# Product-key stage: five small fp32 matmuls get zero rows and unused columns to fill the array

## What is computed

```python
q = (x @ Wq).reshape(b, n, HEADS, DIM) * DIM ** (-0.5)
kv_scores, indices = _pk(x, Wq_pk, pk_keys)      # softmax of the 16 best of 4096 key pairs per token and head
k = jnp.einsum('bnhk,bnhkd->bnhd', kv_scores, keys_table[ind])
v = jnp.einsum('bnhk,bnhkd->bnhd', kv_scores, values_table[ind])
sim = jnp.einsum('bihd,bjhd->bhij', q, k)        # then a causal mask
attn = jax.nn.softmax(sim, axis=-1)
out = jnp.einsum('bhij,bjhd->bhid', attn, v)     # then @ Wo, and added to h
```

## The kernel before

| line | before: rows used, stationary columns, moving columns |
|---|---|
| 1768 | 64 (partitions 64 to 127), 121, 64; twice |
| 1769 | 64, 64, 242 |
| 1775 | 64, 121, 121 and 242 |
| 1801 | 64, 121, 128; four times |
| 1808 | 121, 8, 121 |

## Time and profile before

### The profile page before, as it was taken

How to read it: one execution, slowest core, us unless ns; L and a number is a source line. 1 busy time by engine, 2 the same in 40 slices (tenths; PEclk the granted TensorE clock), 3 DMA queues, 4 the chain that set the end, 5 groups by cost and what they waited for, 6 DMA issues and landing times. The chain is left out here.

```text
span 13713.0 us, 173171 instructions
## 1 busy us (share of the span) xinstructions
PE 9379.0 (68%) x41773; PEld 6076.6 (44%) x41773; DVE 8471.7 (62%) x30632; ACT 5332.5 (39%) x12786; POOL 2229.0 (16%) x2261
## 2 busy tenths in 40 slices
PE   2596799985977999999999999998981010001000
PEld 2486677763863544444444444444971000000000
DVE  7656787665777888888888888886657311111112
ACT  2463466652534555555555555554540000000000
POOL 0000000000000000000000000000000677777774
PEclk6797899997988999999999999998985555555555
DMA  0000000000003333333333333332000432222222
GB/s 5 4 1 2 11 1 4 1 3 2 1 7 90 95 93 98 95 94 93 99 93 95 93 99 93 95 93 58 1 3 19 58 23 22 22 22 26 24 21 39
DMA packets 453151, 616.44 MB, mean 45 GB/s; under 512 B 167514, under 2 KB 420979, under 8 KB 431758
## 3 DMA queue, kind: packets, MB, share of 16 engines
q1 hardware_dynamic: 377490, 566.32, 17.0%
q0 software_dynamic: 74592, 38.28, 4.6%
HBM read 369.09 MB, written 44.81 MB: 30 GB/s over the span
## 5 line engine op out<-in xcount | busy, mean ns | idle before, releaser
L1812 PE MATMUL pm_out<-pm_w,pm_tab 128*128 128x484 f32 x8192 | 4018.1, 571 | 0.9 <-DVE pm_w L2056 0.2
L1917 ACT ACTIVATE pm_e<-pm_sums 128x484 f32<-128x484 f32 x4096 | 2318.4, 574 | 1525.5 <-PE pm_sums L1827 1511.4
L2056 DVE SCALAR_TENSOR_TENSOR pm_w<-pm_sums,pm_e 128x484 f32<-128x484 f32 x4096 | 2661.9, 651 | 148.4 <-ACT pm_e L1917 131.7
L2741 POOL DMA_INDIRECT g_got<-gat_sources,ed_idx x2048 | 1982.5, 968 | 690.4 <-issue 674.3
L1812 PEld LDWEIGHTS pm_out<-pm_w,pm_tab 128*128 128x128 f32 x8192 | 1561.7, 192 | 968.9 <-issue 623.6
L2749 PE MATMUL g_ps<-k_ident,g_xs 121*128 121x121 f32 x32 | 10.7, 437 | 2501.9 <-DVE g_xs L2865 2501.9
L1827 PE MATMUL pm_sums<-pm_mv,pm_pick 96*128 96x484 bf16 x4096 | 1518.3, 371 | 44.9 <-DVE pm_w L2056 24.7
L2878 DVE TENSOR_TENSOR g_e<-g_got,g_b 128x512 f32<-128x512 f32 x16 | 11.1, 692 | 1814.4 <-DMA g_got<-gat_sources,ed_idx 1814.3
L2749 PEld LDWEIGHTS g_ps<-k_ident,g_xs 121*128 121x128 f32 x32 | 5.1, 182 | 2505.1 <-DVE g_xs L2865 2505.0
L113 POOL TENSOR_TENSOR xn<-h,s_st 121x1024 f32<-121x1024 f32 x1 | 2.9, 2937 | 5483.6 <-DVE s_st L94 5483.6
L2810 ACT ACTIVATE g_ex<-g_ex 128x1024 f32<-128x1024 f32 x16 | 16.9, 1056 | 2188.6 <-DVE g_ex L2893 2188.6
(11 more groups left out here) (563 smaller groups left out, 18280.1 us busy)
## 6 DMA issues: line engine op xcount, KB each, us to landing
pm_tab<-in_L_ffn_tables SPq DMA_DIRECT2D x128, 2048.0 KB, 8.0
pm_mv<-pm_parts SPq DMA_DIRECT2D x3072, 60.5 KB, 2.4
g_got<-gat_sources,ed_idx POOLq DMA_INDIRECT x2048, 2.6
pm_gb<-pk_threshold_rows SPq DMA_DIRECT2D x128, 242.0 KB, 7.7
gat_running<-g_rec SPq DMA_DIRECT2D x16, 1536.0 KB, 5.7
gat_expert_rows<-g_y SPq DMA_DIRECT2D x32, 242.0 KB
g_y<-gat_expert_rows SPq DMA_DIRECT2D x4, 1936.0 KB
gat_heads<-ed_same SPq DMA_DIRECT2D x4, 1024.0 KB
```

What stands on the lines that cost most here:

```text
L1812: pe.matmul(out[:, hd % 2, 0:CHUNK], tab[hd % 2][:, t, :], w[:, t % NW, :], start=(t == 0), stop=(t == KT - 1)).then_inc(used, 1)
L1917: a.activation(e[:, t % NW, :], sums[:, t % NB, 0:CHUNK], ACT.Exp).then_inc(exp_ready, 1)
L2056: v.scalar_tensor_tensor(out=w[:, t % NW, :], in0=sums[:, t % NB, 0:CHUNK], scalar=0.0, in1=e[:, t % NW, :], op0=ALU.is_gt, op1=ALU.mult). ...
L2741: g.indirect_dma_start(got[c][:, w, :], None, rows, bass.IndirectOffsetOnAxis(ap=idx[:, i * W + w:i * W + w + 1].bitcast(U32), axis=0)).th ...
```

## The change

Tiles whose matmuls used 64 rows get 128 partitions: `sw`, `xa`, `xc` and `q`. `wo` had 128 already and used its upper half. The added halves are set to zero once, by new memsets in the two `load_all` calls; `wq` gets 64 more columns and `tg` is 128 columns wide instead of 8. The matmuls of the five lines then take all 128 partitions of both operands, or (1808) all 128 columns. Where only one side is zero in the added rows, the other holds finite numbers of another use: `kv` has keys in its lower and values in its upper half. Line 1769 now writes 128 output partitions, of which the upper 64 hold the next head's columns and are read by nobody. All other instructions, their order and their waits stay.

```diff
-        sw = outer.enter_context(nc.sbuf_tensor("pk_sw", [C, NH, 2 * NK], F32))
+        sw = outer.enter_context(nc.sbuf_tensor("pk_sw", [128, NH, 2 * NK], F32))
...
-                [(bd[:, :, :], 0.0)], norm=(k["norm"], h, xn))
+                [(bd[:, :, :], 0.0), (sw[C:128, :, :], 0.0)], norm=(k["norm"], h, xn))
...
-            xb, xa, gb, xc = sb("xb", [KD, CHUNK]), sb("xa", [C, CHUNK]), sb("gb", [128, CHUNK]), sb("xc", [C, CHUNK])
+            xb, xa, gb, xc = sb("xb", [KD, CHUNK]), sb("xa", [128, CHUNK]), sb("gb", [128, CHUNK]), sb("xc", [128, CHUNK])
...
-            tg, tgT, tick = sb("tg", [TP, 2 * TT]), sb("tgT", [2 * TT, TP]), sb("tick", [1, 16])
-            wq, wo = sb("wq", [C, NH * C]), sb("wo", [128, NH, C])
+            tg, tgT, tick = sb("tg", [TP, 128]), sb("tgT", [2 * TT, TP]), sb("tick", [1, 16])
+            wq, wo = sb("wq", [128, NH * C + C]), sb("wo", [128, NH, C])
...
-            q = [sb(f"q{c}", [C, T]) for c in both]
+            q = [sb(f"q{c}", [128, T]) for c in both]
...
-                [(keys[:, :, :], 0.0)])
+                [(ap, 0.0) for ap in (keys[:, :, :], wq[:, :], wo[0:C, :, :], xa[:, :], xc[:, :], tg[:, :], q[0][:, :], q[1][:, :])])
...
                             for t in range(NT):
-                                pe.matmul(X[0:TP, 256 + t * C:256 + (t + 1) * C], kv[c][C:2 * C, t * TP:(t + 1) * TP], wo[C:2 * C, hd, :], start=True, stop=True)
-                            pe.matmul(X[0:C, 0:T], wq[:, hd * C:(hd + 1) * C], xa[:, c * T:(c + 1) * T], start=True, stop=True).then_inc(step[c], 1)
+                                pe.matmul(X[0:TP, 256 + t * C:256 + (t + 1) * C], kv[c][:, t * TP:(t + 1) * TP], wo[:, hd, :], start=True, stop=True)
+                            pe.matmul(X[:, 0:T], wq[:, hd * C:hd * C + 128], xa[:, c * T:(c + 1) * T], start=True, stop=True).then_inc(step[c], 1)
...
                             for t in range(NT):
-                                ins = pe.matmul(Y[0:TP, KEYS[t]], q[c][:, t * TP:(t + 1) * TP], kv[c][0:C, 0:(t + 1) * TP], start=True, stop=True)
+                                ins = pe.matmul(Y[0:TP, KEYS[t]], q[c][:, t * TP:(t + 1) * TP], kv[c][:, 0:(t + 1) * TP], start=True, stop=True)
...
-                        pe.matmul(out[0:2 * TT, bank, 0:TP], tg[:, :], ident[0:TP, 0:TP], start=True, stop=True).then_inc(FI, 1)
+                        pe.matmul(out[:, bank, 0:TP], tg[:, :], ident[0:TP, 0:TP], start=True, stop=True).then_inc(FI, 1)
...
-                            a.activation(q[c][:, :], X[0:C, 0:T], ACT.Copy)
+                            a.activation(q[c][0:C, :], X[0:C, 0:T], ACT.Copy)
```

More of the change, by code:

```diff
@@ L1446, in _ @@
                     a.wait_ge(folded, 1)
-                    a.activation(sw[:, :, :].rearrange("p (b n) k -> p b (n k)", b=2), ps[0][0:C, 0:2, :], ACT.Copy)
+                    a.activation(sw[0:C, :, :].rearrange("p (b n) k -> p b (n k)", b=2), ps[0][0:C, 0:2, :], ACT.Copy)
             xT = sb("xT", [C, M])
@@ L1515, in _ @@
                                 ins = pe.matmul(ps[c][0:TP, 2 * t + q, :], xT[:, c * T + t * TP:c * T + (t + 1) * TP],
-                                                sw[:, 4 * q:4 * q + 4, :].rearrange("p n k -> p (n k)"), start=True, stop=True)
+                                                sw[0:C, 4 * q:4 * q + 4, :].rearrange("p n k -> p (n k)"), start=True, stop=True)
                         ins.then_inc(step[c], 1)
@@ L1629, in stage_l2_ffn @@
                 (mask[:, 0:TP], k["causal"][:, 0, 0:TP]), (mask[:, TP:3 * TP], k["causal"][:, 1, :]), (picks[:, :, :], k["picks"]),
-                (wq[:, :], A["L2_ffn_Wq"]), (wo[C:2 * C, :, :], A["L2_ffn_WoH"].rearrange("n p c -> p n c")),
-                (tab[0][:, :, :], A["L2_ffn_tables"][0]), (xa[:, :], x_rows[:, 0:CHUNK]),
+                (wq[0:C, 0:NH * C], A["L2_ffn_Wq"]), (wo[C:2 * C, :, :], A["L2_ffn_WoH"].rearrange("n p c -> p n c")),
+                (tab[0][:, :, :], A["L2_ffn_tables"][0]), (xa[0:C, :], x_rows[:, 0:CHUNK]),
                 (xb[0:C, :], x_rows[:, 0:CHUNK]), (xb[C:KD, :], t_rows[0, 0:1, 0:CHUNK]),
-                (xc[:, :], x_rows[:, CHUNK:2 * CHUNK])],
-                [(keys[:, :, :], 0.0)])
+                (xc[0:C, :], x_rows[:, CHUNK:2 * CHUNK])],
+                [(ap, 0.0) for ap in (keys[:, :, :], wq[:, :], wo[0:C, :, :], xa[:, :], xc[:, :], tg[:, :], q[0][:, :], q[1][:, :])])
             sums_ready, exp_ready = sem("sums_ready"), sem("exp_ready")
@@ L1727, in body @@
                                 sp.sem_inc(passed, 1)
-                                sp.dma_start(xc[:, :], x_rows[:, CHUNK:M][:, bass.ds(ck * CHUNK, CHUNK)]).then_inc(xc_loaded, 16)
+                                sp.dma_start(xc[0:C, :], x_rows[:, CHUNK:M][:, bass.ds(ck * CHUNK, CHUNK)]).then_inc(xc_loaded, 16)
                             if more:
@@ L1755, in body @@
                                 sp.sem_inc(xa_free, 1)
-                                sp.dma_start(xa[:, :], x_rows[:, bass.ds(ck * CHUNK, CHUNK)]).then_inc(xa_loaded, 16)
+                                sp.dma_start(xa[0:C, :], x_rows[:, bass.ds(ck * CHUNK, CHUNK)]).then_inc(xa_loaded, 16)
                     chunks(sp, body, lambda g, ck: None)
@@ L1985, in _ @@
                     v.tensor_copy(pick[:, :, :], picks[:, :, :]).then_inc(setup, 1)
-                    v.tensor_copy(keys[0:C, :, :], sw[:, :, :])
+                    v.tensor_copy(keys[0:C, :, :], sw[0:C, :, :])
                     v.memset(keys[C:KD, :, NK:2 * NK], 1.0).then_inc(setup, 1)
```

## The result

The changed kernel takes 13478.8 us (median of 4 runs, 13478.2 to 13486.9) against 13704.7 us: a ratio of 0.9836, 95% interval 0.9823 to 0.9849. That is 226 us less; 238.5 were forecast, and the time lies inside the range. The span of the profiled execution is 13476.7 us, 236 less than that of before. The two profiled executions already differ by 12 us ahead of the first added memset (the one before it, of `pk_bd`, starts at 4011.33 and at 3999.39 us), where nothing was changed. So the medians are the better measure of the whole, and the loop's own length that of the edit.

A forecast was written before the change was run, and what follows sets the result against it. TensorE was taken to bound the product-key loop. Savings of 183 us (`q`, `s`) and 59 us (the other two groups), 242 together, less 3.5 us of memsets, gave 238.5 off 13705.3: 13467 us, range 13452 to 13502.

The forecast's parts named there:

- TensorE sets the pace: Product-key loop: TensorE is busy 994 of 1000 us, so every us its stream gains or loses moves the end.
- The cost sits at the edges: Small matmul groups: 0.09 to 0.10 us is paid on entering a group using part of the array, none for full ones.
- The prices of the full array: Four small groups: `q` saves 0.42 us, `s` 0.29 to 0.30, `next_scores` 0.29, `turn_thresholds` 0.20; together 242 us.
- 4 x 0.097 + 2 x 0.203: Group `q`, lines 1768 and 1769: four short records plus two of 242 columns, 0.80 us against 1.22.
- The poor value: Group `q` with paces of 0.11 and 0.21 us: 0.86 us, saving 0.36.
- Nobody takes it back: VectorE's mask waits, 1.13 and 2.51 us, cover TensorE's savings of 0.72 and 1.21; VectorE goes on waiting at every mask.
- The race at t=12: TensorE already waits 0.10 us at t=12, read as for VectorE's `w`; should keep 0.10 us; if lost, 13543 us.
- The memsets: Added before the loads, all on the path: 3.5 us more (2.5 to 5), of which `sw` 0.9.
- Loads stay hidden over all rows: Rival: full-row weight loads wait for the matmul before them, each record pays its load, 13918 us; 2 in 100.
- The granted clock: Rival: filled rows lower TensorE's granted clock to 0.9 in the loop, 560 us on, 14027 us; 1 in 100.
- It doesn't do what it says: Rival: gap comes from output shape or fp32 with few columns, zero rows change nothing, memsets stay: 13709 us; 2 in 100.
- Half of it: Rival: only inner pace improves, 13588 us, or VectorE's race at t=12 is lost, 13543 us; 5 in 100 together.

The follow-up runs named there:

- next_to_s: Kernel before, no tile changed, `next_scores` moved from t=20 to t=21, directly behind lane 1's `s`: 13862.8 us against 13905.3, ratio 0.9970.
- query_first: Changed kernel with line 1769 written before line 1768 in `q`: 13670.1 us against 13907.0 for the kernel before on its chip, ratio 0.9829.
- s_only: Kernel before with the full array for line 1775 (`s`) alone, upper half of `q` tiles zero: 13836.0 us against 13905.3, ratio 0.9950.
- turn_only: Kernel before with line 1808 alone changed, 128 stationary columns instead of 8: 13884.5 us against 13905.3, ratio 0.9984.

## Why the prediction was right, and what was mis-sized

- **TensorE sets the pace**: right. Busy share and waits of the earlier trace rows carried through: the gain of TensorE's stream, 232 us by the groups, is the gain of the loop, 231.4 us.
- **The cost sits at the edges**: right, and next_to_s shows it apart from the zero rows. The entry is 0.09 to 0.10 us, which the prediction read in the earlier trace rows; the rest of the 0.29 us of a group it only priced as a whole. The traces divide it. First `s` in the kernel before, with the weight load (PEld) and, from a view cut so that it begins there, the third record; then the same in the changed kernel:

```profile
6020.91 0.49 PEld L1775 LDWEIGHTS pm_y<-pm_kv,pm_q 64*121 64x121 f32 x4 [0.71 <-issue]
6021.22 0.57 PE L1775 MATMUL pm_y<-pm_kv,pm_q 64*121 64x242 f32 x2
6021.73 0.38 PE L1827 MATMUL pm_sums<-pm_mv,pm_pick 96*128 96x484 bf16 x1
```

```profile
6013.74 0.18 PEld L1775 LDWEIGHTS pm_y<-pm_kv,pm_q 128*121 128x121 f32 x1 [0.22 <-issue]
6014.35 0.57 PE L1775 MATMUL pm_y<-pm_kv,pm_q 128*121 128x242 f32 x2
```

At the edge the first load begins only with its record (6020.91 and 6020.92); without an edge it begins 0.41 us ahead of it (6013.74 and 6014.15). To the third record it takes 0.30 us from the first (6020.92 to 6021.22), and 0.20 without the edge: 0.10 for the load that is no longer hidden. From the third record to line 1827 it takes 0.51 and 0.42 us: 0.09 for leaving. With 0.09 for entering that is the 0.29 us. Why an edge costs this no run shows; that the load waits there is what they show.
- **The prices of the full array**: right for `s`, `next_scores` and `turn_thresholds` to 0.01 us. Wrong for `q`: it saved 0.38 us, not 0.42, 256 x 0.04 = 10 us. The term that was mis-sized is "4 x 0.097 + 2 x 0.203", 0.80 us against 0.84, and in it the query: the four short records took 0.37 us, even less than 0.39, and the two of the query 0.46 where 0.41 was put. The prices came from groups where they do not meet: `pv` is followed by a short bf16 load, and 0.203 is half of a row of ordinary steps. That a long load just behind short records adds 0.05 us was in neither. With the order turned round, query_first measured 0.78 us. The poor value in the prediction (0.86) had it inside.
- **Nobody takes it back**: right. All 256 mask waits of the changed kernel are still there, 321 us together where they were 462. Their sizes were off: 0.57 us where about 0.4 was forecast, 1.93 where about 1.3 was. VectorE also waits for `pv` at line 1960, a wait that the sum of the prediction left out:

```profile
6033.35 0.17 DVE L1960 RECIPROCAL pm_den<-pm_den 121x2 f32<-121x2 f32 x1 [0.76 <-PE pm_y L1786]
```

That is the kernel before; in the changed kernel it is 0.57 us. From the mask of lane 0 to that of lane 1 the trace has two more, both for ScalarE: at line 1979 1.10 us, now 0.99, and at line 2056 0.30 us, now gone. Together the four fell by 1.18 us, and TensorE saved 1.21 in the same stretch. The cover is spread over more waits than the two that were summed. The race at t=12 kept its 0.10 us, as argued.
- **The memsets**: right. VectorE's timeline of the changed kernel shows them, here the first and the last:

```profile
4000.57 0.91 DVE L159 MEMSET pk_sw<- 64x1024 f32 x1 [0.27 <-issue]
...
4145.94 0.91 DVE L159 MEMSET pm_keys<- 65x1024 f32 x1 [5.24 <-PEq L1495]
...
4149.16 0.52 DVE L159 MEMSET pm_q<- 128x242 f32 x2
```

The second chain ends at 4149.68 instead of 4146.85, so 2.8 us, and `sw` adds 0.9: 3.7 us against 3.5.

- **The rivals.** Loads stay hidden over all rows: `s` fell by 0.29 us where that rival had it rise. The granted clock stayed at 1.00 in all four stretches of 1000 us from 5000 to 9000. "It doesn't do what it says" falls with s_only and turn_only. "Half of it" did not come: the entries went to 0.81 or 0.82 us, and the race at t=12 gave nothing back.

With the loop's 231.4 and the memsets' 3.7 the sum is 228 us, and the medians differ by 226.

## What to carry to other kernels

On an engine that sets the pace, look at the distance from a matmul's start to the next, before and after small groups: where it is 0.1 us longer than before full ones, give the small group a 65th row or the missing columns, or put groups of the same shape next to each other. Count edges, not instructions, and those inside a group too: a group that is padded only in part keeps the edge that is left. In this kernel short fp32 records cost 0.05 us less a group ahead of a short bf16 load than ahead of a long fp32 one.

## What the runs showed of the hardware that was not expected

- The step is between 64 and 65 rows: 65 cost as little as 128 (1.64 us in both), 64 cost 1.93.
- Columns count in the same way: with all 128 rows, 64 columns instead of 128 made `q` 0.19 us longer although the load was half as wide.
- The gathers of the last stage follow each other after 1.47 us on two of the chips and after 1.37 on the third, 200 us of a run, while the matmul loop agrees within 1 us (5063.7 and 5064.6).
- At an edge the next weight load begins only with its own record, not 0.4 us ahead of it, and a short run of records costs 0.09 us to enter, 0.10 for that load and 0.09 to leave.
